# The second layer's rectified step-width sum, taken as half of the sums of x and of |x|

## The chip, the cores and the metric

The kernel runs on one core of a Trainium2 chip. The metric is the device time of one execution in microseconds (us). TensorE (PE) multiplies matrices into the eight PSUM banks, ScalarE (ACT) evaluates functions with an optional scale, bias and running sum, VectorE (DVE) and GpSimd (POOL) do element work, SyncE (SP) issues the DMAs. Everything is fp32.

## The reference, cut to what matters

Two layers run one after the other; each is `x = x + attn(layernorm(x)) + ffn(layernorm(x))`, on 4 x 512 tokens of 128 features. The change lies in the second layer's attention, a state-space scan of 256 channels with 16 states, whose step width is one number for each channel, a mean over all tokens:

```python
dt = softplus(einsum('bld,hd->blh', x, W_dt) + b_dt).mean(axis=(0, 1))   # (256,)
dt = clip(dt, 0.001, 2.0)
A = -softplus(A_raw);  A_d = exp(A * dt[:, None])
B_d = (A_d - 1) / (A + 1e-6) * B_ssm
new = A_d * carry + B_d * u_t;  y_t = sum(new * C_ssm)                    # over 512 tokens
```

Here `x` is the layer's normalised input. Both kernels write softplus(p) as max(p, 0) + ln(1 + exp(-|p|)), so that the mean needs two sums over the 2048 tokens: of max(p, 0) and of the logarithm. Since max(p, 0) = (p + |p|) / 2, the first can also be had from the sums of p and |p|.

## The kernel before, in words

The program is written as blocks, one after the other, with an instruction list for each engine and explicit semaphores between them; each engine takes its list in order. A block ends when all engines have ended theirs. The channels of the second layer lie on the partitions, in two halves of 128; a product of one half with the 512 tokens of one batch element is one "unit", so `NU` = 8 units.

`layer0_out` ends the first layer. Its 23 turns are a software pipeline over 16 token tiles of 128: in a turn ACT takes a square root (L1272), copies transposed tiles out of PSUM (L1278, L1280), copies one transposed tile of the second layer's normalised input into `xn1T` (L1288, in 16 of the turns), takes another square root (L1272), and normalises two rows (`yn` L1294, `y2` L1297) that PE transposes in the next turn (L1314, L1317). The copy's semaphore `cp_done` releases POOL's two additions (L1222, L1223) and PE's later turns.

`layer1` is one block. Its lists around the change:

- PE: input products `u_product` (L1573) and gate products `gate_product` (L1579), the expert logits into bank 7 (L1600, then `gate_mm`), turning the expert gates (L1611), then eight `dt_product` (L1585), which alternate between banks 4 and 5, and after them the experts' first products `up` (L1518).
- ACT: gates (sigmoid, L1710), the tiles `u_tile(n)` (L1686, L1690) which DVE's convolution needs, and for each unit an Abs (L1723, kept in `ab`) and a Relu with a running sum (L1726: output `rl` unused, its sum to `dtr`). A running sum makes a second instruction, ACTIVATION_READ_ACCUMULATOR, after the first. Behind the units stand four hidden tiles of the experts (`hidden`, L1679), the last `u_tile`, and then the softplus's exp over all of `ab` (L1737) and two logarithms with running sums into `dtl` (L1742, `ln_done`).
- DVE: convolution and blend of each unit (L1837 to L1853), the expert gates (`gates`, L1796 to L1815), the first half of the inputs' transposition (`turn_inputs(0)`, L1879), then the step width: the sum of `dtr` (L1883), a wait for `ln_done`, the sums L1886 to L1890 and `lna` = A times dt (L1891). The `lna` releases the scan's tables on ACT, a DMA round trip and DVE's own work.
- POOL waits for the second `ln_done` and then clears `region2` (L1980, a memset of 128 x 4096), which held `ab`.

`u_tile(n)` waits in two places for DVE's blend of tile n - 2, whose buffers it takes (`conv_done`, `diff_done`, and `uT_done` ahead of L1690); `dt_product(n)` waits for the Relu of unit n - 2, which frees its bank.

Of the kernel before, what the change touches and what calls it, by code (L numbers as in the profile page):

```python
# [11 lines left out]
ACT = mybir.ActivationFunctionType  # L12
ALU = mybir.AluOpType
AX = mybir.AxisListType.X

P = 128
B, L, D = 4, 512, 128
TOK = B * L
NT = TOK // P
# [11 lines left out]
NE = 8  # L31
# [1152 lines left out]
def layer0_out(nc, a, g):  # L1184
# [5 lines left out]
    sb, sem, con, bank = g["sb"], g["sem"], g["con"], g["bank"]  # L1190
    xt, ffnT, attn_d, xn1, xn1T = g["xt"], g["ffnT"], g["attn_d"], g["xn1"], g["xn1T"]
    wo, wo_bias, up = g["wo"], g["wo_bias"], g["up"]
    with ExitStack() as c:
# [5 lines left out]
        m1 = g["m1"]  # L1199
# [7 lines left out]
        with nc.Block() as block:  # L1207
# [58 lines left out]
            @block.scalar  # L1266
            def _(act):
                for n in range(TURNS):
                    p = n % 2
                    def deviation(part, ks):  # L1270
                        act.wait_ge(var_done, 2 * n + 1 + part)
                        nc.scalar.activation(std[:, p, ks], mv[:, p, ks, 1], ACT.Sqrt, bias=con("eps5")).then_inc(std_done, 1)  # L1272

                    deviation(0, slice(0, 2))
                    if n:
                        act.wait_ge(tr_mm, n)
                        if on(n, 1):
                            ins = nc.scalar.activation(tT[:, p, 0, :], bank[p][:, 0:HD], ACT.Copy)  # L1278
                        if on(n, 4):
                            ins = nc.scalar.activation(tT[:, p, 1, :], bank[p][:, HD:2 * HD], ACT.Copy)  # L1280
                        if n == TURN_W:
                            nc.scalar.activation(m1.wT[:, 0:2, :], bank[2][:, :].rearrange("p (n f) -> p n f", n=2), ACT.Copy)
                        if n == TURN_W + 1:
                            nc.scalar.activation(m1.wT[:, 2, :], bank[3][:, 0:HD], ACT.Copy)
                            nc.scalar.activation(m1.w_outT[:].rearrange("p k d -> p (k d)"), bank[3][:, HD:2 * HD], ACT.Copy)
                        if on(n, 7):
                            i = tile(n - 7)
                            ins = nc.scalar.activation(xn1T[:, i * P:(i + 1) * P], bank[6 + p][:, 0:P], ACT.Copy)  # L1288
                        ins.then_inc(cp_done, 1)
                    deviation(1, slice(2, 3))  # L1290

                    act.wait_ge(rs_done, 3 * n + 2)
                    if on(n, 0):
                        nc.scalar.activation(yn[:, p, :], at[:, tile(n), :], ACT.Identity, bias=shift[:, p, 0:1],  # L1294
                                             scale=rs[:, p, 0:1]).then_inc(act_norms, 1)
                    if on(n, 3):
                        nc.scalar.activation(y2[:, p, :], bank[3 - p][:, 0:HD], ACT.Identity, bias=shift[:, p, 1:2],  # L1297
                                             scale=rs[:, p, 1:2]).then_inc(act_norms, 1)
# [50 lines left out]
class Layer1:  # L1349


    def __init__(self, nc, sb, sem, ffnT, region1):
        self.w_in, self.cleared = sem("l1_weights"), sem("l1_cleared")

        self.gate_w, self.w1 = sb("gate_w", [P, NE]), sb("w1e", [P, 4, P])
        self.w2, self.b1, self.b2 = sb("w2e", [P, 4, D]), sb("b1e", [P, 4]), sb("b2e", [P, D])

        self.region1 = region1
        self.raw = self.region1[:, 0:3 * HD].rearrange("p (n k d) -> p n k d", n=3, k=2)
        self.raw_o = self.region1[:, 3 * HD:4 * HD]  # L1360
        self.wT, self.w_outT = sb("wT", [P, 3, HD]), sb("w_outT", [P, 2, D])
        self.bx, self.bg, self.bd, self.cb = (sb(n, [P, 2]) for n in ("bx", "bg", "bd", "cb"))
        self.cw = sb("cw", [P, 2, 3])
        self.out_b, self.lng, self.lnb = sb("out_b", [P, D]), sb("lng", [P, D]), sb("lnb", [P, D])
        self.a_raw, self.b_ssm, self.c_ssm = (sb(n, [P, 2, NS]) for n in ("a_raw", "b_ssm", "c_ssm"))
        self.win = sb("win", [P, NG, P])
        self.wst = sb("wst", [P, NG, P])
        self.d0 = sb("d0", [P, NG, B, NCH])
        self.kpad = sb("kpad", [P, 4, 2 * TC])
        self.gT = ffnT  # L1370
        self.loads = 0
# [32 lines left out]
def layer1(nc, a, out, g):  # L1404
# [10 lines left out]
    sb, sem, con, bank, m1 = g["sb"], g["sem"], g["con"], g["bank"], g["m1"]  # L1415
    xt, xn1, xn1T, lna_d = g["xt"], g["xn1"], g["xn1T"], g["lna_d"]
    gT, win, wst, d0, kpad, wT, w_outT = m1.gT, m1.win, m1.wst, m1.d0, m1.kpad, m1.wT, m1.w_outT
    a_raw, b_ssm, c_ssm, cw, cb = m1.a_raw, m1.b_ssm, m1.c_ssm, m1.cw, m1.cb
    NBC = B * NCH
    NU = 2 * B  # L1420
    with ExitStack() as c:
# [4 lines left out]
        he = sb("he", [P, 8, 512], c=c)  # L1426
# [6 lines left out]
        ab = region2[:, :].rearrange("p (n l) -> p n l", n=NU)  # L1433
# [18 lines left out]

        z = win[:, 0:NT, :]
        zg = win[:, NT:2 * NT, :]
        rl = he[:, 7, :]
        dtr, dtl = sb("dtr", [P, 2, B], c=c), sb("dtl", [P, 2], c=c)
        dt, t1 = sb("dt", [P, 2], c=c), sb("t1", [P, 2, NS], c=c)
        asp, bsp, lna, cbs = (sb(n, [P, 2, NS], c=c) for n in ("asp", "bsp", "lna", "cbs"))
        lnac, cbc, a32 = sb("lnac", [P, NG], c=c), sb("cbc", [P, NG], c=c), sb("a32", [P, NG], c=c)
# [3 lines left out]
        S = lambda *names: tuple(sem(n, c) for n in names)  # L1463
# [3 lines left out]
        pads, u_mm, g_mm, dt_mm = S("pads", "u_mm", "g_mm", "dt_mm")  # L1467
        u_done, gate_done, conv_done, diff_done, tap_done, uT_done = S(
            "u_done", "gate_done", "conv_done", "diff_done", "tap_done", "uT_done")
        abs_done, relu_done, exp_done, ln_done = S("abs_done", "relu_done", "exp_done", "ln_done")  # L1470

        a_stage, lna_done, t1_done, kex_stage = S("a_stage", "lna_done", "t1_done", "kex_stage")
        v_order, lna_out, lna_in, lnac_done, win_done, a32_done, d0_done = S(
# [9 lines left out]
        half = lambda k: slice(k * P, (k + 1) * P)  # L1483
# [21 lines left out]
        with nc.Block() as block:  # L1505
            @block.tensor
            def _(pe):
                def up(t, q):

                    n = 4 * t + q  # L1510
                    tok = slice(t * 512, t * 512 + 512)
                    if n >= 14:
                        pe.wait_ge(scanned, n - 9)
                    elif n >= 2:
                        pe.wait_ge(he_done, n - 1)
                    else:
                        pe.wait_ge(relu_done, NU - 1 + n)
                    nc.tensor.matmul(up_bank(n)[:, :], m1.w1[:, q, :], xn1T[:, tok], start=True, stop=True).then_inc(up_mm, 1)  # L1518

                def picks(t, qs):  # L1520
# [60 lines left out]
                def dt_product(n):  # L1581
                    b, k = divmod(n, 2)
                    if n >= 2:
                        pe.wait_ge(relu_done, n - 1)
                    nc.tensor.matmul(bank[4 + n % 2][:, :], wT[:, 2, half(k)], xn1T[:, row(b)], start=True, stop=True).then_inc(dt_mm, 1)  # L1585

                def out_product(k, m):
# [10 lines left out]
                gate_product(1)  # L1598
                for i in range(NT):
                    mm = nc.tensor.matmul(bank[7][:, i * NE:(i + 1) * NE], xn1T[:, i * P:(i + 1) * P], m1.gate_w[:], start=True, stop=True)  # L1600
                mm.then_inc(gate_mm, 1)
                gate_product(2)
                gate_product(3)
# [69 lines left out]
            def _(act):  # L1673
# [46 lines left out]
                for n in range(NU):  # L1720
                    b, k = divmod(n, 2)
                    act.wait_ge(dt_mm, n + 1)
                    nc.scalar.activation(ab[:, n, :], bank[4 + n % 2][:, :], ACT.Abs, bias=m1.bd[:, k:k + 1]).then_inc(abs_done, 1)  # L1723
                    if n:
                        act.wait_ge(relu_done, n)
                    nc.scalar.activation(rl, bank[4 + n % 2][:, :], ACT.Relu, bias=m1.bd[:, k:k + 1],  # L1726
                                         accum_out=dtr[:, k, b:b + 1]).then_inc(relu_done, 1)
                    if n in (2, 5):
                        u_tile(4 + n // 5)
                u_tile(6)  # L1730
# [57 lines left out]
            def _(dve):  # L1788
# [3 lines left out]
                def gates():  # L1792

                    logits = bank[7][:, 0:NT * NE].rearrange("p (i e) -> p i e", e=NE)
                    dve.wait_ge(gate_mm, 1)
                    ch.link(nc.vector.tensor_reduce(mx[:], logits, AX, ALU.max))  # L1796
                    nc.vector.tensor_tensor(lg, logits, wide(mx[:, :]), ALU.subtract).then_inc(mx_done, 1)
                    dve.wait_ge(ex_done, 1)
# [78 lines left out]
                def turn_inputs(i):  # L1877
                    half_n = slice(i * NBC // 2, (i + 1) * NBC // 2)
                    nc.vector.transpose(v[:, :, half_n].rearrange("p j n -> p n j"),  # L1879
                                        uT[:, :, i * TOK // 2:(i + 1) * TOK // 2].rearrange("p k (n r) -> p n k r", r=TC)).then_inc(v_done, 1)  # L1880

                turn_inputs(0)
                w(nc.vector.tensor_reduce(dt[:], dtr[:], AX, ALU.add))  # L1883
                dve.wait_ge(ln_done, 2)
                dve.wait_ge(a_stage, 3)
                sc.mark(nc.vector.tensor_tensor(asp[:], bsp[:], asp[:], ALU.add))  # L1886
                w(nc.vector.tensor_tensor(dt[:], dt[:], dtl[:], ALU.add))
                sc.mark(nc.vector.tensor_scalar(asp[:], asp[:], -1.0, None, ALU.mult))  # L1888
                w(nc.vector.tensor_scalar(dt[:], dt[:], 1.0 / TOK, 0.001, ALU.mult, ALU.max))
                w(nc.vector.tensor_scalar(dt[:], dt[:], 2.0, None, ALU.min))  # L1890
# [127 lines left out]
```

## Time and profile before

| | |
|---|---|
| median of 3 runs | 437.49 us (435.13 to 437.85) |
| the profiled execution's own time | 435.33 us |
| its span, first to last instruction | 433.5 us |
| PE / DVE / ACT / POOL busy, share of the span | 87 / 70 / 65 / 39 % |
| mean granted TensorE clock | 0.947 of full speed |
| the layer0_out turns | 242 to 294.46 us of the span |
| layer1 | 294.46 us to the end |

The busy shares are means over stages with different limits. What matters for the change is which wait ends last between 294 and 351 us, and how the turns before it are chained. Times in the rows below are counted from the span's start.

### The profile page before, as it was taken

The page shows a single profiled execution, that of the slowest core. Times are in us where ns is not written, and L with a number is a line of the kernel's source. Part 1 is how long each engine was busy: PE and PEld are TensorE (multiplying, and loading weights), DVE is VectorE, ACT ScalarE, POOL GpSimd, SP SyncE. Part 2 cuts the span into 40 slices and gives each one's busy share as a digit, 9 for nine tenths or more (in the row PEclk, how much of TensorE's full clock was granted, in tenths as well). Part 3 has the DMA queues.
Part 4 walks back from the last instruction along what each step waited for, and adds up shares of the span by engine and source line. Part 5 has one row for each costly group of instructions (what it writes and reads, how often), then busy time and mean ns, then how long its engine had stood idle before and what let it go on. Part 6 is the DMA issues. An engine that isn't in the chain of part 4 may idle for free. (4 is left out here: it accounts for less than half of the span.)

```text
span 433.5 us, 10054 instructions
## 1 busy us (share of the span) xinstructions
PE 375.8 (87%) x3136; PEld 260.3 (60%) x3136; DVE 304.4 (70%) x1005; ACT 281.8 (65%) x691; POOL 168.6 (39%) x269
## 2 busy tenths in 40 slices
PE   1999999997999999999977999969788659688993
PEld 0454344366777777778764777766242435666982
DVE  4666809743998898889945578766989795374195
ACT  4687768473666666666627466646599942995634
POOL 1403919202788888888859032332000030000013
PEclk9999999998999999999999799989799688898997
DMA  8320323262122222222246100000000010000003
GB/s 230 60 81 9 107 73 106 60 176 79 45 76 76 73 73 73 73 73 63 65 153 148 23 1 2 0 2 0 1 2 1 0 27 2 1 2 0 2 0 98
DMA packets 33148, 23.14 MB, mean 53 GB/s; under 512 B 10062, under 2 KB 32860, under 8 KB 33116
## 3 DMA queue, kind: packets, MB, share of 16 engines
q1 hardware_dynamic: 31868, 22.67, 19.1%
q8 instruction: 16, 0.26, 0.3%
q10 hardware_dynamic: 1248, 0.07, 0.2%
q14 instruction: 16, 0.13, 0.1%
HBM read 13.26 MB, written 9.47 MB: 52 GB/s over the span
## 5 line engine op out<-in xcount | busy, mean ns | idle before, releaser
L486 PE MATMUL psum<-w,hT 128*128 128x385 f32 x128 | 45.5, 496 | 0.6 <-ACT stage L613 0.4
L900 PE MATMUL psum<-win,wst 128*32 128x128 f32 x1024 | 38.1, 279 | 1.3 <-ACT kd L975 1.3
L486 PEld LDWEIGHTS psum<-w,hT 128*128 128x128 f32 x128 | 23.2, 189 | 25.1 <-issue 11.4
L1004 ACT ACTIVATE std<-mv,cst 128x2 f32<-128x2 f32 (+1 forms) x34 | 10.0, 296 | 40.8 <-DVE mv L1142 38.4
L995 ACT ACTIVATE win<-psum 128x512 f32<-128x512 f32 x62 | 35.7, 581 | 0.0
L900 PEld LDWEIGHTS psum<-win,wst 128*32 128x32 f32 x1024 | 28.7, 110 | 5.6 <-ACT kd L975 1.5
L1272 ACT ACTIVATE std_<-mv_,cst 128x2 f32<-128x2 f32 (+1 forms) x46 | 13.5, 296 | 28.3 <-DVE mv_ L1250 16.4
L1500 POOL TENSOR_TENSOR win<-win,lng 128x512 f32<-128x512 f32 x2 | 2.5, 1272 | 71.2 <-ACT win L1785 71.2
L1057 POOL TENSOR_SCALAR xh<-raw,mv,rs 128x128 f32<-128x128 f32 x32 | 25.4, 795 | 3.2 <-DVE rs L1118 2.7
L1050 POOL TENSOR_TENSOR xkm<-win,wst 128x256 f32<-128x256 f32 x32 | 19.6, 614 | 15.3 <-PE psum L918 9.3
L1518 PE MATMUL psum<-xn1T,w1e 128*128 128x512 f32 x32 | 18.8, 714 | 7.7 <-ACT he L1679 6.1
L1222 POOL TENSOR_TENSOR xn<-xn,out_b 128x128 f32<-128x128 f32 x16 | 7.3, 454 | 42.6 <-ACT xn1T L1288 42.6
L1980 POOL MEMSET region<- 128x4096 f32 x1 | 3.5, 3512 | 50.6 <-ACT region L1742 50.6
L612 ACT ACTIVATE stage<-psum 128x384 f32<-128x384 f32 x32 | 15.7, 489 | 10.8 <-PE psum L486 9.4
L918 PE MATMUL psum<-grad,xkm 32*128 32x128 f32 x496 | 22.5, 296 | 0.0
L1045 POOL TENSOR_TENSOR cc<-win,wst 128x128 f32<-128x128 f32 x32 | 13.8, 432 | 21.6 <-POOLq L299 20.2
L1334 PE MATMUL psum<-region,tT 128*128 128x256 f32 x64 | 19.4, 429 | 0.0
L1542 PE MATMUL psum<-w2e,he 128*128 128x128 f32 x128 | 19.1, 298 | 0.0
L918 PEld LDWEIGHTS psum<-grad,xkm 32*128 32x128 f32 x496 | 16.6, 185 | 3.7
L910 PE MATMUL psum<-grad,masks 128*128 128x128 f32 x62 | 15.0, 324 | 3.9 <-DVE grad L1166 2.2
L1542 PEld LDWEIGHTS psum<-w2e,he 128*128 128x128 f32 x128 | 18.0, 217 | 0.0
L1679 ACT ACTIVATE he<-psum,b1e 128x512 f32<-128x512 f32 x16 | 10.5, 681 | 10.2 <-PE psum L1518 10.2
(307 smaller groups left out, 1142.4 us busy)
## 6 DMA issues: line engine op xcount, KB each, us to landing
rows_scratch<-stage SPq DMA_DIRECT2D x32, 192.5 KB
win<-rows_scratch SPq DMA_DIRECT2D x32, 192.5 KB, 2.4
attn_scratch<-ob SPq DMA_DIRECT2D x32, 64.0 KB
att<-attn_scratch SPq DMA_DIRECT2D x4, 512.0 KB, 4.0
xt<-in_L_attn_x SPq DMA_DIRECT2D x4, 256.0 KB, 4.2
out<-win SPq DMA_DIRECT2D x4, 256.0 KB, 2.4
cst<-in_constants SPq DMA_DIRECT2D x1, 408.0 KB, 5.1
w<-in_L_attn_wk SPq DMA_DIRECT2D x2, 128.0 KB, 4.2
```

The lines of the kernel that those rows point to most:

```text
L486: mm = nc.tensor.matmul(rows_bank(i, h)[:, 0:RC], hT[:, k, i * P:(i + 1) * P], w4[:, k, h, :], start=(k == 0), stop=(k == 1))
L612: act.activation(stage[:, i % 2, h, 0:3 * F], src[:, 0:3 * F], ACT.Copy).then_inc(stage_done[h], 1)
L900: mm = nc.tensor.matmul(dst[32 * b:32 * b + 32, 0:F], v[:, at:at + 2 * K], w_sb[:, state, first_slot(b) + h, :], start=False, stop=(h == 1 ...
L910: nc.tensor.matmul(zbanks[(p + 1) % 2][:, 0:F], masks[:, (p + 1) % RING, P:2 * P], g_t, start=False, stop=True, skip_group_check=True).the ...
L918: mm = nc.tensor.matmul(bank[b][:, h * F:(h + 1) * F], xkm[own, p % 2, h, :], grad[own, p % 2, :], start=False, stop=False, skip_group_che ...
L995: nc.scalar.activation(own, psum[:, 2 * half:2 * half + 2, 0:H * F].rearrange("p b (h g) -> p b h g", h=H), ACT.Copy).then_inc(w_done, 1)
L1045: nc.gpsimd.tensor_tensor(cc[:, p % 2, :], rows[:, p, F:2 * F], ggb[:], ALU.add).then_inc(cc_done, 1)
L1050: nc.gpsimd.tensor_tensor(xkm[:, p % 2, :, :], rows[:, p, 0:F][:, None, :].broadcast_to([P, H, F]), headt[:, :, None].broadcast_to([P, H, ...
L1057: nc.gpsimd.tensor_scalar(xh[:], raw[:, p, :], mv2[:, p % 2, 0, 0:1], rs2[:, p % 2, 0:1], ALU.subtract, ALU.mult).then_inc(xg_done, 1)
L1334: ins = nc.tensor.matmul(dst, tT[:, 1 - p, 0, k * P:(k + 1) * P], wo[:, k, :], start=False, stop=(k == 1))
L1518: nc.tensor.matmul(up_bank(n)[:, :], m1.w1[:, q, :], xn1T[:, tok], start=True, stop=True).then_inc(up_mm, 1)
L1542: mm = nc.tensor.matmul(dst, he[:, (4 * t + q) % 8, i * P:(i + 1) * P], m1.w2[:, q, :], start=False, stop=(q == 3))
```

## The change

ACT's Abs now has the running sum itself (into `dtr`), and the eight Relu with their accumulator reads are gone, and with them `relu_done` and `rl`; a `dt_product` and the first two `up` now wait for the Abs. The sum of p over the tokens is made from sums of the inputs: the copy into `xn1T` in `layer0_out` becomes an Identity with a running sum into a new tile `sums` (128 features x 16 tiles), two small products of `W_dt` with `sums` follow the expert logits on PE, into the same bank, and DVE reduces them (`dts`) at the head of `gates`. The step-width chain on DVE gets a wait for the last Abs, an addition of `dts` and one of 2048 times the bias ahead of the wait for `ln_done`; the addition of `dtl` behind that wait becomes a scalar_tensor_tensor that halves the first sum too.

```diff
@@ layer0_out, ACT
-  ins = nc.scalar.activation(xn1T[:, i * P:(i + 1) * P], bank[6 + p][:, 0:P], ACT.Copy)
+  ins = nc.scalar.activation(xn1T[:, i * P:(i + 1) * P], bank[6 + p][:, 0:P], ACT.Identity,
+                             accum_out=m1.sums[:, i:i + 1])
@@ Layer1
+  self.sums = sb("x_sums", [P, NT])
@@ layer1
-  rl = he[:, 7, :]
+  dts = sb("dts", [P, 2], c=c)
@@ PE: up(0, 0) and up(0, 1)
-  pe.wait_ge(relu_done, NU - 1 + n)
+  pe.wait_ge(abs_done, NU - 1 + n)
@@ PE: dt_product
-  pe.wait_ge(relu_done, n - 1)
+  pe.wait_ge(abs_done, n - 1)
@@ PE, behind the expert logits
+  for k in range(2):
+      mm = nc.tensor.matmul(bank[7][:, (NE + k) * NT:(NE + k + 1) * NT], wT[:, 2, half(k)], m1.sums[:], start=True, stop=True)
   mm.then_inc(gate_mm, 1)
@@ ACT, for each unit n
-  nc.scalar.activation(ab[:, n, :], bank[4 + n % 2][:, :], ACT.Abs, bias=m1.bd[:, k:k + 1]).then_inc(abs_done, 1)
-  if n:
-      act.wait_ge(relu_done, n)
-  nc.scalar.activation(rl, bank[4 + n % 2][:, :], ACT.Relu, bias=m1.bd[:, k:k + 1],
-                       accum_out=dtr[:, k, b:b + 1]).then_inc(relu_done, 1)
+  nc.scalar.activation(ab[:, n, :], bank[4 + n % 2][:, :], ACT.Abs, bias=m1.bd[:, k:k + 1],
+                       accum_out=dtr[:, k, b:b + 1]).then_inc(abs_done, 1)
@@ DVE, gates()
   dve.wait_ge(gate_mm, 1)
+  ch.mark(nc.vector.tensor_reduce(dts[:], bank[7][:, NE * NT:(NE + 2) * NT].rearrange("p (k i) -> p k i", k=2), AX, ALU.add))
   ch.link(nc.vector.tensor_reduce(mx[:], logits, AX, ALU.max))
@@ DVE, behind turn_inputs(0)
+  dve.wait_ge(abs_done, NU)
   w(nc.vector.tensor_reduce(dt[:], dtr[:], AX, ALU.add))
+  w(nc.vector.tensor_tensor(dt[:], dt[:], dts[:], ALU.add))
+  w(nc.vector.scalar_tensor_tensor(out=dt[:], in0=m1.bd[:], scalar=float(TOK), in1=dt[:], op0=ALU.mult, op1=ALU.add))
   dve.wait_ge(ln_done, 2)
   dve.wait_ge(a_stage, 3)
   sc.mark(nc.vector.tensor_tensor(asp[:], bsp[:], asp[:], ALU.add))
-  w(nc.vector.tensor_tensor(dt[:], dt[:], dtl[:], ALU.add))
+  w(nc.vector.scalar_tensor_tensor(out=dt[:], in0=dt[:], scalar=0.5, in1=dtl[:], op0=ALU.mult, op1=ALU.add))
```

## Rows read from the trace of the kernel before

**Rows 1.** Windows view: busy us (instructions) of PE, PEld, DVE, ACT, POOL; granted clock; DMA.

```profile
318.15:346.90 28.75, 21.95 (x75) 10.50 (x74) 25.95 (x36) 28.23 (x43) 0.03 (x1) 0.88 0.00 0
...
370.80:374.20 3.40, 2.95 (x14) 2.95 (x15) 0.40 (x1) 3.35 (x5) 0.00 (x0) 0.51 0.00 0
```

**Rows 2.** Groups by line and shape, ACT: busy us, mean ns, then idle before.

```profile
L1726 ACT ACTIVATE he<-psum,bd 128x512 f32<-128x512 f32 x8 | 5.5, 683 | 0.0
L1288 ACT ACTIVATE xn1T<-psum 128x128 f32<-128x128 f32 x16 | 4.4, 276 | 0.0
```

**Rows 3.** Timeline (start us, us, instruction, idle before and releaser), step-width units, 316 to 331 us.

```profile
316.58 0.67 ACT L1723 ACTIVATE region<-psum,bd 128x512 f32<-128x512 f32 x1
...
317.15 0.67 ACT L1726 ACTIVATE he<-psum,bd 128x512 f32<-128x512 f32 x1
...
317.72 0.19 ACT L1726 ACTIVATION_READ_ACCUMULATOR he<-psum,bd 128x1 f32 x1
317.81 0.68 ACT L1723 ACTIVATE region<-psum,bd 128x512 f32<-128x512 f32 x1
...
319.44 0.69 ACT L1723 ACTIVATE region<-psum,bd 128x512 f32<-128x512 f32 x1 [0.28 <-PE psum L1585]
...
323.53 1.13 PE L1585 MATMUL psum<-xn1T,wT 128*128 128x512 f32 x2 [1.46 <-ACT he L1726]
...
324.69 0.69 ACT L1723 ACTIVATE region<-psum,bd 128x512 f32<-128x512 f32 x1
...
327.19 0.69 DVE L1853 TENSOR_TENSOR uT<-region 128x512 f32<-128x512 f32 x1
...
330.58 0.82 ACT L1690 ACTIVATE region<-region,cb,cw 128x512 f32<-128x512 f32 x1
```

**Rows 4.** Timeline, softplus and step-width chain, 337 to 351 us.

```profile
337.87 3.62 ACT L1737 ACTIVATE region<-region 128x4096 f32<-128x4096 f32 x1
...
341.08 3.71 DVE L1879 STREAM_TRANSPOSE region<-uT 128x2048 f32<-128x2048 f32 x1
...
344.64 0.15 DVE L1883 TENSOR_REDUCE dt<-dtr 128x2 f32<-128x8 f32 x1
...
346.87 3.51 POOL L1980 MEMSET region<- 128x4096 f32 x1 [50.59 <-ACT region L1742]
346.90 0.19 DVE L1886 TENSOR_TENSOR asp<-bsp,asp 128x32 f32<-128x32 f32 x1 [2.11 <-issue]
...
347.20 3.21 DVE L1888 TENSOR_SCALAR asp<-asp 128x32 f32<-128x32 f32 x1
...
350.67 0.19 DVE L1891 TENSOR_TENSOR lna<-asp,dt 128x32 f32<-128x32 f32 x1
```

**Rows 5.** Timeline, one turn of layer0_out in its steady part, 272 to 276 us.

```profile
272.80 0.44 PE L1314 MATMUL psum<-cst,yn 128*128 128x128 f32 x2
...
274.53 0.28 ACT L1288 ACTIVATE xn1T<-psum 128x128 f32<-128x128 f32 x1
...
274.69 0.30 ACT L1272 ACTIVATE std_<-mv_,cst 128x1 f32<-128x1 f32 x1
...
275.22 0.61 DVE L1263 TENSOR_SCALAR xn<-xt,mv_,rs 128x128 f32<-128x128 f32 x1
...
275.98 0.44 PE L1314 MATMUL psum<-cst,yn 128*128 128x128 f32 x2
```

**Rows 6.** Timeline, expert logits and gates, 298 to 314 us.

```profile
298.02 3.63 PE L1600 MATMUL psum<-gate_w,xn1T 128*128 128x8 f32 x32
...
306.36 0.31 ACT L1715 ACTIVATE he<-he 128x128 f32<-128x128 f32 x1 [3.82 <-DVE he L1797]
...
308.84 5.40 PE L1579 MATMUL psum<-xn1T,wT 128*128 128x512 f32 x8 [2.82 <-ACT region L1710]
```

**Rows 7.** Timeline, an experts' second product at either clock, 371 to 377 us.

```profile
371.84 1.92 PE L1542 MATMUL psum<-w2e,he 128*128 128x128 f32 x8
...
376.30 1.06 PE L1542 MATMUL psum<-w2e,he 128*128 128x128 f32 x8
```

More of the change, by code:

```diff
@@ L1454, in layer1 @@
         zg = win[:, NT:2 * NT, :]
-        rl = he[:, 7, :]
-        dtr, dtl = sb("dtr", [P, 2, B], c=c), sb("dtl", [P, 2], c=c)
+        dtr, dtl, dts = sb("dtr", [P, 2, B], c=c), sb("dtl", [P, 2], c=c), sb("dts", [P, 2], c=c)
         dt, t1 = sb("dt", [P, 2], c=c), sb("t1", [P, 2, NS], c=c)
@@ L1469, in layer1 @@
             "u_done", "gate_done", "conv_done", "diff_done", "tap_done", "uT_done")
-        abs_done, relu_done, exp_done, ln_done = S("abs_done", "relu_done", "exp_done", "ln_done")
+        abs_done, exp_done, ln_done = S("abs_done", "exp_done", "ln_done")
         a_stage, lna_done, t1_done, kex_stage = S("a_stage", "lna_done", "t1_done", "kex_stage")
```

## The prediction

> **What bounds the kernel now.** I read the windows view first, by stage. Between 318 and 347 us ACT is busy for 28.23 of 28.75 us and DVE for 25.95, PE for 21.95 [rows 1]. So work taken from ACT can shorten this stage, but DVE stands close behind. The groups by line give the price of what goes: eight Relu of 683 ns [rows 2]. The timeline and the waits then say what these 28 us end in. ACT works without a break up to the softplus's second logarithm. Its accumulator read releases two things at once: POOL's memset of 3.51 us, at 346.87, and DVE's step-width chain at 346.90, which had idled for 2.11 us. DVE's first tensor_scalar, issued at 347.20 on 32 columns, then takes 3.21 us and ends at 350.41, just behind the memset's end at 350.38; `lna` follows at 350.67 [rows 4]. The reader is to see that `lna` hangs on ACT through the memset: logarithm, memset, tensor_scalar, `lna`. A gain on ACT arrives there whole, as long as DVE is at its wait before the memset ends.
>
> On the memset the Trainium skill agrees (SBUF — State Buffer, section Who interferes with whom): whichever of DVE in a two-port mode and GpSimd issues first has the shared ports for its whole instruction, and the other is blocked. The 3.21 us of the row [rows 4] are such a block.
>
> **Removed: eight Relu on ACT.** The Abs starts at 316.58, the Relu at 317.15, the next Abs at 317.81: 0.57 us from start to start without an accumulator read, 0.66 with one [rows 3]. The read itself lasts 0.19 but costs the next instruction only 0.09. The read moves to the Abs, so 8 x 0.57 = 4.56 us of ACT's issue time go. Not all arrives; I walk the units.
> - Unit 2's Abs at 319.44 waited 0.28 us for its product [rows 3]. PE's list ahead of that product holds nothing that waits for a Relu, so this start stays; the two Relu before it (1.14) turn into waiting.
> - Behind it Relu 2, 3 and 4 go, 1.71 us, but unit 5's product waits for unit 3's sum, in the bank that it takes over. Before, PE started at 323.53 on Relu 3's read, and the Abs followed at 324.69 [rows 3]. Unit 3's Abs is 0.57 earlier and releases 0.57 sooner, so the product and Abs 5 come 1.14 us earlier. Here 0.57 is lost.
> - Relu 5, 6, 7 give 1.71 more: 2.85 at `u_tile(6)`. Its second half, at 330.58, needs DVE's blend of tile 4, which ends at 327.19 + 0.69 = 327.88 [rows 3]. With 0.05 for the semaphore it starts at 327.93 and no sooner: 2.65 us earlier. From there to the logarithms ACT's list is contiguous and I find no wait on DVE or PE that comes later than ACT.
>
> The exp over `ab` moves from 337.87 to 335.22, the logarithms' release from 346.87 to 344.22, the memset's end to 347.73 and `lna` to 348.02 [rows 4]: **-2.65 us**. DVE's own list does not move, since it has no idle time from 319 us on. It ends the transposition at 341.08 + 3.71 = 344.79, and its first sum starts at 344.64 with 0.15 us [rows 4]. The two added small operations take about 0.2 each with their waits (nearest row: the 0.19 us addition at 346.90), so DVE is at its `ln_done` wait near 345.25, after the release but 2.5 us before the memset ends. The added operations and the new wait for the last Abs are therefore free; the memset hides them. Without that cover `lna` could be at 346.2. Behind the Abs wait DVE queues only the step-width chain, and its last Abs lies 15 us back. Not in the trace: a memset of POOL beside DVE's transposition, which it would meet from 344.22 to 344.79. If it had to wait, 0.57 of the gain goes; I take none, since DVE's additions at 346.90 ran beside it undisturbed, and keep 2.1 as the lower end. Upper end: the full 4.56.
>
> By the SBUF page's rule an instruction with one SBUF input outside the two-port modes doesn't meet GpSimd at all; by it the transposition costs the memset nothing and the sum stays as it is.
>
> What follows on `lna` (ACT's exps, DVE's tables, the DMA round trip) is queued behind it or released by it, so I carry the 2.65 us to the end.
>
> **Added: a sum at 16 copies in `layer0_out`.** In a steady turn ACT copies `xn1T` at 274.53 and takes the square root at 274.69. That root releases DVE's normalisation (275.22), and behind it stand `yn` and `y2`, for which PE's next turn waits: 272.80 to 275.98, 3.18 us a turn [rows 5]. So the copy lies on the loop's path. The kind (Identity without a bias) I price as the Copy: the Exp of 128 x 128 without a bias took 0.31 us [rows 6] against 0.276 [rows 2]. The read delays what follows by 0.09 [rows 3]. In steady turns the loop through `y2`, PE's products and DVE's statistics takes two turns to close, so each turn pays half, 10 x 0.045 = 0.45; in the last six turns, with fewer stages, the normalisation goes straight to PE and back: 6 x 0.09 = 0.54. POOL's additions wait for the same copy and shift alike. Together **+1.0 us**. Ends: 16 x 0.045 = 0.7 where the one-turn loop has room throughout, and 16 x (0.19 + 0.03) = 3.5 where the root waits for the whole read. The row nearest is the pitch of 0.09, as here too an independent instruction follows. A gain I exclude: nothing is taken out of the turns.
>
> By the Trainium skill (ScalarE: Activation LUTs, What ACT_TABLE_LOAD costs) each pointer operand adds about 93 ns; if the Identity read a zero bias that way, an estimate of 16 x 0.093 = 1.5 us would be the most it adds. No row here has an Identity without bias.
>
> **Added: the small products and their reduction.** Two fp32 products are four PE instructions; 32 with the logits' shape took 3.63 us [rows 6], so 0.45 us, or 0.9 at half clock. They delay `gate_mm` and two gate products, but PE later waits 2.82 us for ACT at 308.84 [rows 6]: nothing, and 0.45 if that cover were gone. The reduction on DVE stands ahead of the exp for which ACT idled 3.82 us [rows 6], and PE's 2.82 wait hangs on that ACT work: on the path, and ahead of all the later stage. Nearest row: 0.15 us for 128 x 8 [rows 4]; without a wait behind it I take 0.12 (0.1 to 0.3). **+0.1 us**.
>
> **Sum.** -2.65 + 1.0 + 0.1 = -1.55. The profiled execution took 435.33, so 433.8 in its terms. It lies 2.2 us below the median of the three runs; from the median 437.49 the forecast is **436.0**.
>
> **Rivals.**
> - *ACT's whole saving arrives.* If PE's products and DVE's blends run closer than I walked them, `lna` comes 4.5 us earlier (DVE ready at 345.25 just allows it): -4.5 + 1.1 = -3.4, 434.1. For it: ACT is the busiest engine of the stage [rows 1]. Against: the 0.28 wait at 319.44 and the product at 323.53 that waits for ACT [rows 3].
> - *The read costs its length on the turns' path: slower.* The accumulator read has to end before the root starts, and there is no half turn of slack: 16 x 0.22 = 3.5. Then -2.65 + 3.5 + 0.1 = +0.95, 438.4. It decides from (2.65 - 0.1) / 16 = 0.16 us a turn on. For it: the turns chain ACT, DVE and PE closely [rows 5]. Against: the pitch of 0.66 behind a read [rows 3].
> - *The granted clock falls elsewhere.* At 371 us, behind an idle PE, the clock was 0.51 for 3.4 us and eight of the experts' products took 1.92 us against 1.06 at full clock [rows 1, 7]. The change moves PE's idle times, longer ahead of 341 us and shorter ahead of 354. One such stretch more or less on the path is 3.4 / 2 = 1.7 us: 437.7 or 434.3.
> - *DVE holds all.* If POOL's memset did not set `lna`, DVE's list would; it is at 345.25 against 346.90, so 1.65 would remain of the gain: -0.55, 436.9.
>
> **How the numbers follow.** Forecast 0.50, whole saving 0.13, slower by the read 0.12, clock 0.20 (half each way), DVE 0.05. The cases' middles run from 434.1 to 438.4; the three runs of before spread over -2.4 and +0.4 around their median, and a median of a few runs inherits part of that. Range 432.6 to 438.8. About 1%, 4.4 us, is what a measurement of this kernel tells from no change. Faster by more needs the whole saving or the clock's gain together with a low base: 0.14. Slower by more needs the read's full price and a clock lost: 0.04. Within: 0.82.
>
> **What would show it.** In the changed profile: no L1726 group, eight accumulator reads behind the Abs; Abs 2 still waiting for PE; the memset and `lna` 2.65 us closer to the block's start, and the first tensor_scalar still ending with the memset; DVE without idle time between the transposition and the step width; turns 0.05 to 0.1 us longer. I would be wrong if the turns grow by 0.16 or more, if ACT's second half of `u_tile(6)` doesn't end up waiting for DVE, or if PE's or DVE's work behind `lna` stays where it was.

## The result, and the profile after

Over 20 executions of each kernel the changed one has a median of 435.94 us (431.41 to 437.74) and the one before 435.28 (428.88 to 438.58). The ratio is 1.0078, with a 95% interval of 1.0044 to 1.0112: slower by 0.4 to 1.1%, where the forecast was faster by 0.3%. The ratio compares executions within 1.5% of each kernel's fastest, which leaves out ten of the 20 of before and none of the changed kernel's; the means of all 20 differ by 0.5 ± 1.7 us. Everywhere below a time without another name is therefore a mean over all executions, with one standard error: before 433.85 ± 0.22 (172 executions in five sets), changed 435.10 ± 0.43 (32 in two sets). The difference is +1.2 ± 1.0 us (95%), where the sum said -1.55.

The profiled execution took 437.05 us, with a span of 435.2 and a granted clock of 0.944, against 433.5 and 0.947. I split both spans at four events: the first and the last copy into `xn1T`, ACT's first tile of `layer1`, and `lna`.

| us | start to first copy | first to last copy | to first tile | tile to `lna` | `lna` to the end |
|---|---|---|---|---|---|
| before | 248.86 | 44.04 | 2.80 | 54.97 | 82.86 |
| changed | 250.30 | 44.96 | 2.84 | 52.59 | 84.48 |

In this pair of traces the two stages that the change edits moved nearly as forecast, +0.9 (forecast 1.0) and -2.4 (forecast -2.55). The first and the last stage, in which it edits nothing, took +1.4 and +1.6. Now the rows, first those of the edited stages.

ACT's groups by line and shape of the changed kernel (busy us, mean ns, then idle before):

```profile
L1726 ACT ACTIVATE region<-psum,bd 128x512 f32<-128x512 f32 x8 | 5.4, 675 | 2.0 <-PE psum L1586 2.0
L1288 ACT ACTIVATE xn1T<-psum 128x128 f32<-128x128 f32 x16 | 4.4, 276 | 0.0
L1288 ACT ACTIVATION_READ_ACCUMULATOR xn1T<-psum 128x1 f32 x16 | 3.3, 208 | 0.0
L1726 ACT ACTIVATION_READ_ACCUMULATOR region<-psum,bd 128x1 f32 x8 | 1.5, 192 | 0.0
```

The Relu are gone. Abs with a sum lasts what it lasted without one (675 ns, against 0.67 to 0.69 us in [rows 3]), and Identity without a bias lasts the 276 ns of the Copy [rows 2]. What the units lost on ACT comes back in part as a wait of 2.0 us for `dt_product`, now L1586.

The timeline of the changed kernel's units, with the blend of tile 4 on DVE:

```profile
322.05 0.69 ACT L1726 ACTIVATE region<-psum,bd 128x512 f32<-128x512 f32 x1 [1.44 <-PE psum L1586]
...
326.14 0.69 ACT L1726 ACTIVATE region<-psum,bd 128x512 f32<-128x512 f32 x1 [0.55 <-PE psum L1586]
...
329.80 0.69 DVE L1854 TENSOR_TENSOR uT<-region 128x512 f32<-128x512 f32 x1
...
330.59 0.81 ACT L1693 ACTIVATE region<-region,cb,cw 128x512 f32<-128x512 f32 x1
```

This is the walk of the units: unit 2's Abs waits 1.44 us for its product, where it had waited 0.28 [rows 3] (the forecast was 0.28 + 1.14 = 1.42), unit 5's waits 0.55 (forecast 0.57), and the second half of `u_tile(6)` starts 0.10 us behind the blend's end at 330.49 (forecast 0.05).

The timeline of the changed kernel's chain to `lna`, and the head of the expert gates:

```profile
308.13 0.18 DVE L1796 TENSOR_REDUCE dts<-psum 128x2 f32<-128x32 f32 x1
308.23 0.28 DVE L1797 TENSOR_REDUCE mx<-psum 128x16 f32<-128x128 f32 x1
...
343.69 3.73 DVE L1880 STREAM_TRANSPOSE region<-uT 128x2048 f32<-128x2048 f32 x1
...
346.88 3.51 POOL L1984 MEMSET region<- 128x4096 f32 x1 [48.20 <-ACT region L1742]
347.27 0.15 DVE L1885 TENSOR_REDUCE dt<-dtr 128x2 f32<-128x8 f32 x1
...
347.87 0.19 DVE L1890 TENSOR_TENSOR asp<-bsp,asp 128x32 f32<-128x32 f32 x1
...
348.17 2.25 DVE L1892 TENSOR_SCALAR asp<-asp 128x32 f32<-128x32 f32 x1
...
350.69 0.19 DVE L1895 TENSOR_TENSOR lna<-asp,dt 128x32 f32<-128x32 f32 x1
```

The small reduction costs 0.10 from start to start. Counted from ACT's first tile (298.10 here, 295.70 before), the memset starts at 48.78 instead of 51.17, and the first tensor_scalar ends at 350.42, 0.03 behind the memset (346.88 + 3.51), as in [rows 4]. DVE reaches its wait 1 us behind the logarithms, as the sum had it, and the memset covers that: the tensor_scalar shrinks from 3.21 to 2.25 us, and its end stays with the memset's. The transposition (3.73) and the memset (3.51), which now meet for half a microsecond, last what they lasted apart. `lna` stands 52.59 us behind the tile, 2.38 earlier (forecast 2.65 - 0.1 = 2.55).

The timeline of `layer0_out`: PE at the start of a turn and two turns later, first in the kernel before,

```profile
263.15 0.44 PE L1314 MATMUL psum<-cst,yn 128*128 128x128 f32 x2
...
269.57 0.44 PE L1314 MATMUL psum<-cst,yn 128*128 128x128 f32 x2
```

then in the changed kernel, with one copy:

```profile
261.84 0.44 PE L1315 MATMUL psum<-cst,yn 128*128 128x128 f32 x2 [0.28 <-ACT y L1298]
263.40 0.28 ACT L1288 ACTIVATE xn1T<-psum 128x128 f32<-128x128 f32 x1
263.56 0.21 ACT L1288 ACTIVATION_READ_ACCUMULATOR xn1T<-psum 128x1 f32 x1
263.65 0.30 ACT L1272 ACTIVATE std_<-mv_,cst 128x1 f32<-128x1 f32 x1
...
268.35 0.44 PE L1315 MATMUL psum<-cst,yn 128*128 128x128 f32 x2 [0.28 <-ACT y L1298]
```

The read of 0.21 us delays the root by 0.09 (0.25 behind the copy's start, against 0.16 in [rows 5]). Two turns take 6.51 us, where they took 6.42 before. That is the 0.045 a turn.

Now the stage behind `lna`, PE's timeline with one row of DVE, of the kernel before:

```profile
354.47 6.69 PE L1518 MATMUL psum<-xn1T,w1e 128*128 128x512 f32 x8 [4.74 <-ACT he L1679]
361.09 1.14 PE L1531 MATMUL psum<-ffnT,cst 2*128 2x512 f32 x8
...
362.49 1.06 PE L1542 MATMUL psum<-w2e,he 128*128 128x128 f32 x8
...
364.72 1.06 PE L1542 MATMUL psum<-w2e,he 128*128 128x128 f32 x8
...
366.93 0.69 DVE L1831 TENSOR_TENSOR xt<-xt,psum 128x512 f32<-128x512 f32 x1 [3.89 <-PE psum L1542]
```

and of the changed kernel:

```profile
354.48 3.89 PE L1519 MATMUL psum<-xn1T,w1e 128*128 128x512 f32 x8 [2.31 <-ACT he L1682]
361.05 1.14 PE L1532 MATMUL psum<-ffnT,cst 2*128 2x512 f32 x8 [2.68 <-DVE he L1826]
...
362.45 1.60 PE L1543 MATMUL psum<-w2e,he 128*128 128x128 f32 x8
...
364.27 1.91 PE L1543 MATMUL psum<-w2e,he 128*128 128x128 f32 x8
...
368.52 0.69 DVE L1832 TENSOR_TENSOR xt<-xt,psum 128x512 f32<-128x512 f32 x1 [5.55 <-PE psum L1543]
```

The windows of the kernel before over these two steps (busy us of PE, PEld, DVE, ACT, POOL; then the granted clock),

```profile
354.50:361.00 6.50, 6.50 (x8) 2.40 (x8) 6.33 (x14) 2.56 (x4) 0.00 (x0) 0.54 0.10 27
361.10:366.70 5.60, 5.60 (x49) 4.84 (x49) 0.80 (x2) 0.69 (x1) 0.00 (x0) 1.00 0.01 3
```

and of the changed one:

```profile
354.50:361.00 6.50, 3.87 (x8) 1.25 (x8) 6.33 (x14) 3.26 (x5) 0.00 (x0) 1.00 0.10 29
363.00:366.30 3.30, 3.30 (x17) 3.30 (x17) 0.00 (x0) 0.00 (x0) 0.00 (x0) 0.52 0.00 0
```

`lna` stands at 350.67 and 350.69, so the times compare directly. Before, PE had idled for 4.74 us, and the experts' first products ran at a clock of 0.54 for 6.69 us. That cost nothing: DVE was busy for 6.33 of these 6.50 us, and the next step on PE (the picks, 361.09) waits for DVE anyway. The second products then ran at full speed. In the changed kernel the chain ahead is shorter, PE's idle time is 2.31 us, and the same products run at full speed in 3.89. They only end sooner; PE idles 2.68 us for DVE, and the picks start at 361.05 as before. Then the clock falls to 0.52 over the second products, for which DVE sits idle: 5.55 us instead of 3.89, and its addition comes 1.6 us later. In this pair of traces the half-clock time has moved from a covered place to one on the path. What that is worth in the mean of many executions is a matter for the experiments.

### The profile page after: what moved, and what is told of

Its sections match the earlier page's. It is cut to its first block and busy times, and to the rows that moved or that the text cites. A ratio compares the mean times of both kernels' runs of the same rounds, so it can differ in the third digit from the quotient of the medians.

```text
span 435.2 us, 10073 instructions
## 1 busy us (share of the span) xinstructions
PE 377.0 (87%) x3140; PEld 263.1 (60%) x3140; DVE 303.7 (70%) x1008; ACT 278.7 (64%) x699; POOL 168.8 (39%) x269
## 5 line engine op out<-in xcount | busy, mean ns | idle before, releaser
L1543 PE MATMUL psum<-w2e,he 128*128 128x128 f32 x128 | 20.7, 316 | 0.0
L1335 PE MATMUL psum<-region,tT 128*128 128x256 f32 x64 | 20.7, 452 | 0.0
L1543 PEld LDWEIGHTS psum<-w2e,he 128*128 128x128 f32 x128 | 19.5, 233 | 0.0
L1519 PE MATMUL psum<-xn1T,w1e 128*128 128x512 f32 x32 | 15.9, 612 | 4.1 <-ACT he L1682 3.2
```

The source lines that it names most:

```text
L1335: ins = nc.tensor.matmul(dst, tT[:, 1 - p, 0, k * P:(k + 1) * P], wo[:, k, :], start=False, stop=(k == 1))
L1543: mm = nc.tensor.matmul(dst, he[:, (4 * t + q) % 8, i * P:(i + 1) * P], m1.w2[:, q, :], start=False, stop=(q == 3))
```

## The experiments

Half-clock time below means stretches of the windows view with a clock near 0.5. A chain is "short" where the Relu are gone. For an execution without a profile, (1 - mean clock) x span is the clock time that it lost.

**The changed kernel and the one before again**, in the same set, to see what of the four stages repeats.

> The kernel before, unchanged, once more, for a second trace of it. Theory A (the steps hold, the granted clock makes the rest): the interval holds 1.00, and the stretches that hold none of the change move between this trace and the first one of the same kernel by 1 to 3 us, wherever the half-clock stretches of 3.4 us differ; from layer1's first ACT tile to lna 55.0 us as before (54.97), and the turns with a copy into xn1T 44.4 us from the first square root of turn 7 to that of turn 22, both within 0.3. Theory B (the clock stretches lie the same way in every execution of one kernel, so that the change itself moved them): from turn 7 back and from lna on the two traces of before agree within 0.5 us.

> The changed kernel, unchanged, once more, for a second trace of it. Theory A: from layer1's first ACT tile to lna 52.6 us again (0.3), the turns 45.4 us from turn 7 to turn 22, and the stretch from lna to the end anywhere between 81.5 and 85 us. Theory B: from lna to the end 84.5 again, within 0.5, as the granted clock is down over the experts' second product behind lna in each execution.

Measured: before again 433.77 ± 0.8, ratio 1.0021 (0.9972 to 1.0070); changed again 435.31, ratio 1.0037 (0.9996 to 1.0077). The stages of their profiles: before again 244.2, 43.5, 2.8, 56.3, 82.9; changed again 247.5, 46.0, 3.8, 51.6, 84.4. The stage ahead of the first copy differs by 4.6 us between two traces of before, so the +1.4 there is no effect that two traces can show. The stage behind `lna` repeats in these two pairs, and so does its row (windows of the changed kernel again; its `lna` is at 348.99):

```profile
360.40:363.70 3.30, 3.30 (x19) 3.19 (x16) 0.69 (x1) 0.00 (x0) 0.00 (x0) 0.50 0.02 5
```

**The sums at the copies alone**: the kernel before with only the copies changed, the sums unused; run twice.

```diff
-  ins = nc.scalar.activation(xn1T[...], bank[6 + p][:, 0:P], ACT.Copy)
+  ins = nc.scalar.activation(xn1T[...], bank[6 + p][:, 0:P], ACT.Identity, accum_out=m1.sums[:, i:i + 1])
```

> The kernel before, and of the change only the running sum at the 16 copies into xn1T; nothing uses the sums. Theory A: the turns from 7 to 22 take 0.9 us longer than before (0.7 to 1.1), layer1 is as before (55.0 us from its first ACT tile to lna); in time +0.9 us, ratio 1.002. The rival that the read costs its length on the path: 3.5 us more in the turns, ratio 1.008.

> The kernel before with only the running sum at the 16 copies, once more. If the 2.4 us that it cost were the reads (0.9 in the turns) and the clock's chance, its mean now lies 0 to 2 us above before's and the stretch from the first to the last copy is 0.8 to 1.0 us longer where no half-clock stretch falls into it; if the reads cost more than the turns' trace shows, 2 to 3 us again.

Measured: ratios 1.0094 (1.0049 to 1.0140) and 1.0107 (1.0056 to 1.0159); 437.15 ± 0.55 over both, +3.3 ± 1.2 (95%) to before. That is the size of the rival (1.008) and not of the steps (1.002). The copies in the traces (source view: shortest, median and longest in ns, then the first and the last start), of before again, then of the two runs:

```profile
L1288 ACT ACTIVATE xn1T<-psum x16: 268/277/283, 244.2 to 287.7; 128x128 f32<-128x128 f32 x16
...
L1288 ACT ACTIVATE xn1T<-psum x16: 267/277/284, 251.5 to 295.8; 128x128 f32<-128x128 f32 x16
...
L1288 ACT ACTIVATE xn1T<-psum x16: 267/277/285, 248.1 to 292.5; 128x128 f32<-128x128 f32 x16
```

None of the three has a half-clock stretch between its first and its last copy (the first traces of before and of the changed kernel have one each, at their last copies). From first to last copy they take 43.5, 44.3 and 44.4 us: the sums cost 0.9 there, as forecast. So the price in an execution is larger than what the turns show.

**The shorter chain alone**: the changed kernel with plain copies; the `sums` tile is zero, so the sum of the inputs is left out of the step width, all else is done.

```diff
-  ins = nc.scalar.activation(xn1T[...], ..., ACT.Identity, accum_out=m1.sums[:, i:i + 1])
+  ins = nc.scalar.activation(xn1T[...], ..., ACT.Copy)
+  nc.gpsimd.memset(self.sums[:], 0.0)        # in Layer1.clear
```

> The changed kernel, but the 16 copies stay plain copies without a sum, and the sums' tile holds zeros, so the step width lacks the sum of the inputs. Theory A: turns as before, layer1 2.4 us shorter from its first ACT tile to lna (52.6), and in time 2.4 us faster, ratio 0.9945, give or take the clock. Theory B: lna 2.4 us earlier too, but the stretch behind lna 1.6 us longer than in the traces of before, ratio 0.998.

Measured: 431.42 ± 0.87, ratio 0.9922 (0.9883 to 0.9962), -2.4 ± 2.0 (95%) to all of before. The tile-to-`lna` stage is 52.4, the stage behind it 84.5, with the half-clock stretch in the same place (windows of this kernel, `lna` at 343.32):

```profile
355.00:358.30 3.30, 3.30 (x16) 3.30 (x17) 0.65 (x1) 0.00 (x0) 0.00 (x0) 0.50 0.00 0
```

So the stretch comes from the shorter chain and not from the copies. The time shows no loss by it: -2.4 is what Theory A expected, and the ratio leaves out Theory B's 0.998, though the traces look as Theory B said. The changed kernel against the copies alone gives the chain's price a second time, -2.0 ± 1.4. This kernel also holds the new `sums` tile, so the tile's place in memory is not what costs the copies their 3.3.

**Ten unused products in PE's new idle time**, the test of the clock: 2.4 us of PE's time ahead of the picks, which wait for DVE there. First in the changed kernel.

```diff
   up(t, 1)
+  if t == 2:
+      keep_warm(nc, bank[1][:, 0:P], con("ident"), 10)
   picks(t, range(4))
```

> The changed kernel with ten more fp32 products of 128 x 128 on PE, unused, into bank 1 ahead of the experts' third row of picks, where PE idles 2.7 us in the changed kernel. Theory B (the change takes a half-clock stretch from PE work that DVE covers and puts it on the experts' second product behind lna, which the end waits for): the clock stays full there, its four groups take 4.7 us instead of 6.3, from lna to the end 82.8 us instead of 84.5; in time 1.5 us less than the changed kernel, ratio to the kernel before about 0.998. Rival (the 1.7 us behind lna come by chance of the stretches): lna to the end stays between 84 and 85, or moves as often up as down, and the mean clock is no higher.

Measured: 433.12 ± 0.79, ratio 1.0015 (0.9963 to 1.0067), -2.0 ± 1.9 (95%) to the changed kernel. PE's timeline of this kernel, whose `lna` is at 348.8, with the unused products at L753:

```profile
352.59 3.89 PE L1519 MATMUL psum<-xn1T,w1e 128*128 128x512 f32 x8 [2.19 <-ACT he L1684]
356.32 2.39 PE L753 MATMUL psum<-cst 128*128 128x128 f32 x20
359.16 1.14 PE L1532 MATMUL psum<-ffnT,cst 2*128 2x512 f32 x8 [0.44 <-DVE he L1828]
...
360.55 1.06 PE L1543 MATMUL psum<-w2e,he 128*128 128x128 f32 x8
361.67 1.06 PE L1543 MATMUL psum<-w2e,he 128*128 128x128 f32 x8
```

The picks stand where they stood, 10.4 us behind `lna`, and the second products behind them have their 1.06 us. `lna` to the end takes 81.2 us in this trace, not the 82.8 expected: with the stretch at 12 us behind `lna` those at 22 and 46 are gone too. No run puts the ten products into the kernel before, so this doesn't yet show that the gain belongs to the change.

**The sums of the inputs made on PE instead**, to have the change without the reads in the turns: plain copies, and 17 products with a column of ones in an idle time of PE, where `xn1` is at hand.

```diff
...
+  if t == 1:
+      pe.wait_ge(u_done, NU)
+      for i in range(NT):
+          nc.tensor.matmul(bank[1][:, 0:1], xn1[:, i, :], con("ones")[:, 0:1], start=(i == 0), stop=False)
+      nc.tensor.matmul(bank[1][:, 0:1], m1.out_b[:], m1.neg[:], start=False, stop=True).then_inc(xs_mm, 1)
   picks(t, range(4))
...
```

> The changed kernel with plain copies into xn1T; the sums of the inputs come from 16 products of the normalised input with a column of ones on PE (and one that takes the added output bias off), placed in PE's idle time ahead of the experts' second picks, one small copy on DVE, and two products behind the picks. If the reads cost what the turns' trace shows: turns 43.5 to 44.0 us as before, lna 2.3 us earlier than in the kernel before, in time 0.9 us less than the changed kernel; if the reads cost more than the turns show (2.4 us, as reads_alone measured), 2.4 us less than it, ratio 0.995.

> Both edits: sums on PE and the ten unused products ahead of the third picks. Theory B: another 1.5 us less than sums_on_pe, ratio to the kernel before about 0.991 to 0.993, lna to the end 82.8. Rival: as sums_on_pe.

Measured: without the ten unused products 434.79 ± 0.62, ratio 1.0087 (1.0038 to 1.0137); with them 431.32 ± 0.89, ratio 0.9947 (0.9898 to 0.9995). The products take 3.5 ± 2.3 us (95%) off. The first missed what I expected: 0.3 ± 1.6 us below the changed kernel instead of 0.9 or 2.4, and 3.4 ± 2.2 above the chain alone, which has the same short chain and plain copies. No run shows why. In its trace the stretch is there again (windows, `lna` at 345.85):

```profile
358.70:362.00 3.30, 3.30 (x17) 3.30 (x17) 0.00 (x0) 0.00 (x0) 0.00 (x0) 0.50 0.00 0
```

With the products there is none in that place, but two in a row 43 us behind `lna`, and `lna` to the end takes 84.5 us without and with them, where 82.8 was expected with them. So the traces of this pair don't show the gain.

**The four with the clock kept up**: unused products in eight idle times of PE, in `layer0_out`'s first and last turns and in `layer1`. The change, its copies alone and its chain alone are then compared with the kernel before. The products are the same in all four, but for two neighbouring places in `layer1`: 14 and 18 with the old chain, 25 and 9 with the short one.

```diff
+  if n <= 5: keep_warm(nc, bank[7][:, 0:P], con("ident"), 5)             # layer0_out
+  elif n > NT: keep_warm(nc, bank[1 - p][:, 0:P], con("ident"), 3)
+  keep_warm(nc, bank[6][:, 0:P], con("ident"), 12)                       # layer1, behind u_product(2)
+  pe.wait_ge(u_done, NU)
+  keep_warm(nc, bank[0][:, 0:P], con("ident"), 14)   # ahead of picks(1); 25 with the short chain
...
```

> The kernel before, with unused fp32 products of 128 x 128 on PE in eight of its idle times (first five turns of layer0_out, turns 17 to 20, ahead of the fifth gate product, around the experts' second and third rows and ahead of the scan's outputs), the same places in all four kernels of this set, so that the clock has less reason to fall. Both theories: fewer half-clock stretches, mean clock 0.975 or more, and the executions lie closer together than the 10 us of the kernel before. It is the base of the set.

> The changed kernel with the same unused products. With the clock out of the way the steps alone stand: -2.4 in layer1 and +0.9 in the turns, so 1.5 us faster than before_warm (1 to 2). If instead the reads cost 2.4 us or more, as reads_alone and reads_again measured: within 0.5 of before_warm or slower.

> reads_alone (the kernel before with the sums at the 16 copies, unused) with the same unused products. Steps: 0.9 us slower than before_warm (0.7 to 1.1). If the reads cost more than the turns show: 2 us or more.

> abs_alone (the changed kernel without the 16 sums, the sum of the inputs left out of the step width) with the same unused products. Steps: 2.4 us faster than before_warm, and after_warm lies 0.9 above this one.

| | as it is, us | to the first row (95%) | with the products | to the first row (95%) | forecast step | mean clock, without and with |
|---|---|---|---|---|---|---|
| before | 433.85 ± 0.22 | | 432.78 ± 0.42 | | | 0.956, 0.986 |
| changed | 435.10 ± 0.43 | +1.2 ± 1.0 | 430.46 ± 0.29 | -2.3 ± 1.1 | -1.55 | 0.951, 0.988 |
| copies alone | 437.15 ± 0.55 | +3.3 ± 1.2 | 433.54 ± 0.33 | +0.8 ± 1.1 | +1.0 | 0.953, 0.985 |
| chain alone | 431.42 ± 0.87 | -2.4 ± 2.0 | 430.40 ± 0.50 | -2.4 ± 1.4 | -2.55 | 0.960, 0.985 |

With the clock kept up the change is faster, and each forecast step lies within its interval. Each part can be read twice in either column, once with and once without the other part. The copies cost 3.3 and 3.7 us as they are, 3.5 ± 1.2 on the mean, and 0.8 and 0.1 with the products, 0.4 ± 0.8. The chain gains 2.4 and 2.0, 2.2 ± 1.2 on the mean, and 2.4 and 3.1 with the products, 2.7 ± 0.8. So the products take 3.1 ± 1.4 us off the price of the copies, and what they change at the chain, 0.5 ± 1.4, can't be told from nothing. (`lna` to the end takes 82.2, 82.2, 81.2 and 82.1 us in the traces of the four, in the table's order.)

The changed kernel with these products has the lowest mean of the kernels that compute everything: 3.1 ± 1.2 us (95%) below the kernel before as it is, in the same set. The ratio, taken as the first paragraph says, is 0.9982 (0.9945 to 1.0020), within what can't be told from no change. The ratios of the other three are 1.0041 (1.0000 to 1.0082), 1.0075 (1.0036 to 1.0114) and 0.9972 (0.9929 to 1.0015).

**The copies with the clock kept up in one block only**, to place what they cost beyond the turns: only the products in `layer0_out`, or only those in `layer1`, each in the kernel before and with the copies changed.

> The kernel before with the unused products in layer0_out alone (first five turns, turns 17 to 20). Base for the next: no half-clock stretch between 225 and 290 us; the stretches of layer1 as in the kernel before.

> reads_alone with the same. If the excess of the reads over the 0.9 us in their turns comes from half-clock stretches in layer0_out: 0.5 to 1.5 us above before_warm_turns. If it comes from layer1's stretches: 2 to 3.5 us above it still.

> The kernel before with the unused products in layer1 alone (ahead of the fifth gate product, around the experts' second and third rows, ahead of the scan's outputs). Base for the next: stretches in layer0_out as in the kernel before, at most one or two in layer1 ahead of the end.

> reads_alone with the same. If the excess comes from half-clock stretches in layer1: 0.5 to 1.5 us above before_warm_layer1. If it comes from layer0_out: 2 to 3.5 us above it.

Measured, with and without the changed copies: 435.36 ± 0.67 against 434.32 ± 0.39 with the products in `layer0_out`, +1.0 ± 1.6; 434.85 ± 0.53 against 432.26 ± 0.46 with those in `layer1`, +2.6 ± 1.5. The excess seems to go where `layer0_out`'s clock is kept up and to stay where only `layer1`'s is, but the two intervals overlap: this points to `layer0_out` and doesn't settle it.

## Why the prediction was wrong

- **The step that failed is the "+1.0 us" for the sum at 16 copies.** It was read off the turns, and there it is right: 0.09 behind each copy, 0.045 a turn, 0.9 for the stage. In executions the same edit costs 3.5 ± 1.2 us. With the clock kept up it costs 0.4 ± 0.8, so the excess goes with the unused products, which keep PE's clock up; for the clock the sum held nothing. The lost clock time gives a rough estimate: the copies alone lost 20.61 us of it and before 18.85, the changed kernel 21.30 and the chain alone 17.24. At the 0.58 us of the last section, which was fitted within kernels and not between them, the differences make 1.0 and 2.4, and with the 0.9 of the turns 1.9 and 3.3, against 3.3 ± 1.2 and 3.7 ± 2.1 measured. That fits the clock as the cause and doesn't prove it.
- **Where the copies' excess falls stays open.** The runs with one block kept up point to `layer0_out`. In the traces the stretches of `layer0_out` stand mostly in its first turns, ahead of the first changed copy, and their number differs between traces of one kernel, so single traces can't show a shift in their mean.
- **The rival "the read costs its length" had the right sign and size by luck.** Its 3.5 us were to come from a root that waits for the whole read. The root starts 0.09 later, not 0.21. The price of a pointer operand (the Trainium skill, ScalarE: Activation LUTs, What ACT_TABLE_LOAD costs) doesn't show either: the Identity takes the Copy's 276 ns.
- **The walk of the units and the chain to `lna`: right.** 2.38 us earlier against 2.55, with each wait within 0.05 us of the forecast, and the memset still ends the tensor_scalar. The 0.57 us kept back for a memset beside the transposition were not lost. By the rule of the Trainium skill that I cited (SBUF — State Buffer, Who interferes with whom) a DVE instruction with one SBUF input outside the two-port modes doesn't meet GpSimd; the trace agrees for the transposition, with 3.73 and 3.51 us against 3.71 and 3.51 apart [rows 4].
- **The reduction in the gates: right**, 0.10 for 0.1. The small products show no cost.
- **"So I carry the 2.65 us to the end" is not refuted by the times, but the traces tell against it.** The chain's gain is 2.2 ± 1.2 us in executions, and the whole 2.55 lies within that. In the four traces with the short chain and no products in the gap, `lna` to the end took 84.4 to 84.5 us each time, with a half-clock stretch that begins 11 to 13 us behind `lna`. In the six traces with the old chain and nothing added in `layer1` (before, its repeat, the two with the copies alone, the two with products in `layer0_out` only) no such stretch stands there. Yet three of them took 84.5 too, with two stretches in a row near 43 us; two took 82.9, with one at 20 or 21 and one at 44 or 45, and one took 81.2, with none from 10 to 50. So the short chain's stage is longer by 1.6 us against the first pair of profiles, and by 1.1 ± 1.4 (95%) against the mean of the six (83.4): not clear of noise. The ten unused products take off 2.0 ± 1.9 in one pair and 3.5 ± 2.3 in the other, but which stretches that pays for isn't shown.
- **The clock was among the rivals, but as chance.** I gave it half a chance each way, "longer ahead of 341 us and shorter ahead of 354", and one price of 1.7 us. The runs show a loss that came with the edit: the eight sets of products take 3.6 ± 1.3 and 4.6 ± 1.1 us off the two kernels with the changed copies, and 1.1 ± 1.0 and 1.0 ± 2.1 off the two with plain ones. None of the signs that I named for being wrong came up, and none of them looked at the clock.

So of the 2.8 us between -1.55 and +1.2, the copies take 2.5 ± 1.2 and the chain 0.3 ± 1.2. The absolute forecast (437.49 - 1.55 = 435.94, written 436.0) meets the measured median by luck: the median of three from which it started stood 2.2 us above that of twenty.

## What to carry to other kernels

Measure the parts of a change alone and together, as the kernel is and with unused products in PE's idle times. That tells an edit's own price from the clock time that comes with it, and it points at another part than the traces did: here the stage that looked worst in the profile cost nothing that the times can show, and the part whose steps were priced right cost 2.5 us more. Look, too, for half-clock stretches that lie under another engine's work, since the trace shows one come out on the path when the idle time ahead of it shrank. Use many executions, for traces of one kernel differ by several us in stages that nobody has touched.

## What was unexpected of the hardware

Over the 352 executions of all these kernels that have a clock on record, each microsecond of lost clock time cost 0.58 ± 0.03 us within one kernel (a fit with a level for each kernel; the lost time runs from 3 to 31 us), so most of the spread of one kernel's times, 428.4 to 438.9 us for the one before, goes with the clock. Between kernels this price doesn't hold: the unused products took 13 us of lost clock time from the kernel before, and its time fell by 1.1 ± 1.0 us only; whether those stretches were covered or the products cost time themselves, no run tells. And an accumulator read of 0.21 us behind a copy, or 0.19 behind a Relu or an Abs, holds up the next instruction on ACT by 0.09 us only, with an Identity without bias at the price of a Copy, 276 ns for 128 x 128.
